# A four-stage residual block on one core: five exchanges of order, and the copies of the key pages moved to later unit steps

## The chip, the core and the metric

One NeuronCore of a Trainium2 chip runs the whole program. The metric is the device time in microseconds, the median of several executions. Each profiled execution is a single one; its span runs from the first to the last instruction.

## What is computed

x has shape (8, 128, 512). Four stages are added to it, one after the other. The part of the reference that matters here:

```
x = x + L0(x)   # SwiGLU MLP, F = 1376, with LoRA adapters of rank 16 per sequence
x = x + L1(x)   # attention: 32 query heads, 8 key heads, D = 128, 512 cached keys
                # gathered from pages by block_table, and 128 new keys
x = x + L2(x)   # 512 x 512 weight, quantised by a codebook, with LoRA
x = x + L3(x)   # 512 x 512 weight chosen per sequence

q = rope(rmsnorm(x Wq)); k = rope(rmsnorm(x Wk)); v = x Wv
kc = k_cache[block_table]; vc = v_cache[block_table]        # 16 pages of 32 keys
probs = softmax(where(valid, q k^T * D**-0.5, -1e30)); o = probs v
out = o Wo
```

## The kernel before

Every fp32 product is made of three products in the faster fp32r format: each operand is split into a high half (ScalarE, ACT, copies it with rounding) and a low half (VectorE, DVE, or GpSimd, POOL, subtracts). TensorE (PE) multiplies high by high, high by low and low by high.

Each of the five engines runs its own instruction list, written out by hand as Python calls in the order of issue, and waits for counts of semaphores. Nothing is scheduled by a tool, so the order of the calls is the order on the engine. The fifth engine, SP, computes nothing: it issues DMAs, one after the other, and a wait in its list holds back all that stand behind.

**The MLP** works in 11 blocks of the hidden width for each half of the sequences. For a block n, `high_w(n)` and `low_w(n)` split the weights, `high_wb` and `low_wb` the adapters, `silu` and `gated` make the activation and `high_act`, `low_act` split it. `mask_t` and `low_t` prepare the products of the adapters (tile `tb`), for which TensorE waits in `lora_out`. `angles` makes the rotary angles, which are needed later.

**The attention** works in 64 units: unit k is key head k // 8 of sequence k % 8, with its four query heads. The engines are software-pipelined: in step u, TensorE projects unit u (`project_q`, `project_kv`), turns and applies the probabilities of unit u - 2 (`transpose_p`, `attend`), makes scores of units u - 1 and u, and ends with `output(u - 2)`, which reads `oTh` and `oTl`. `transpose_queries` and `transpose_new` turn the rotated queries and the new keys. The first three units (`first`, `second`, `third`) are written out by hand, since they overlap the end of the MLP.

The probabilities are not divided by their sums; the output is. For this the four inverses of each row have to be laid across the partitions, and they go through DRAM: `invert` on DVE makes `inv`, SP's `put_inv` stores it in `inv_dram` (2 KB), SP's `spread_inv` waits for that store and broadcasts it to all partitions (`inv_row`, 256 KB), ACT's `lay_inv` copies it into the order of the output (`inv_wide`), DVE's `norm_o` multiplies, and ACT's `high_o` makes `oTh`. ACT has `square_q`, `scale_k` and `high_o` behind `lay_inv`, all in the order of the list.

The cached keys and values are first copied page by page from the cache into DRAM buffers in the order of the sequences (128 pages of 128 KB for the keys, on SP; `copy_keys(n)` issues the next n). Each page has its index read from SBUF into registers, and then its DMA. Units 0 to 7 wait for the 16 pages of their sequence in `load_k`; later heads read the same buffers. 92 of the 128 pages are issued before the first unit step of SP, `step(0)`, and the rest between the other DMAs of the steps 0 to 6: `load_v`, `load_rope`, `load_k` (four DMAs), and in step 4 four weight loads of the next head (`load_next_in`). The DVE engine turns the loaded keys in `turn_cached_k`, ACT makes their high half in `high_cached_k`.

**The last two stages** go sequence by sequence; `add3(b)` adds the third stage's result into x, after which TensorE turns it (`turn_x3`), and `low_w3_part` splits a quarter of the last weights.

Of the kernel before, what the change touches and what calls it, by code (L numbers as in the profile page):

```python
# [24 lines left out]
B, T, HID = 8, 128, 512  # L25
# [17 lines left out]
KC = KEYS // P  # L43
SPLIT = KEYS // 2
PUT_SCALES = 32
QW = REP * D
QKV = QW + 2 * D
DEPTH = 4
# [80 lines left out]
def cond_resid_kernel(nc, ins, out):  # L129
    ctx = ExitStack()  # L130
    with ctx:
# [218 lines left out]
        def _(sp):  # L350
# [153 lines left out]
            first = Unit(0)  # L504
# [38 lines left out]
            def spread_inv(u):  # L543
                if u.exists():
                    sp.wait_ge(S["inv_put"], u.count(16, 16))
                    sp.dma_start(inv_row[:, :], inv_dram[u.k % 2].rearrange("t h -> (t h)").partition_broadcast(P)
                                 ).then_inc(S["inv_in"], 16)

            def step(u):
                put_inv(u + -2)  # L550
                if u.k == 2:
                    spread_inv(u + -2)
                    copy_keys(2)
                else:
                    if u.k < B - 1:
                        copy_keys(2)
                    spread_inv(u + -2)
                if (u + -1).exists() and u.k > 1:
                    load_v(u + -1)
                if (u + 1).exists():  # L560
                    load_rope(u + 1)
                    load_k(u + 1)
                load_next_in(u)
                load_next_out(u)
                if u.k < B - 1:
                    copy_keys(4 if u.k else 2)

            def load_w3(b):
                if b >= 2:
# [15 lines left out]
            for n in range(2):  # L585
                cols = slice(n * HID // 2, (n + 1) * HID // 2)
# [188 lines left out]
        def _(act_e):  # L775
# [168 lines left out]
            for n in range(1, FC):  # L944
                if n >= 3:
                    high_w(n + 1)
                high_act(n - 1)
                if n == FC - 1:
                    copy_delta(0)
                if n >= 3:  # L950
                    high_wb(n + 1)
                if n == 7:
                    sines()
                    act_e.wait_ge(S["idx_in"], 64)
                    act_e.activation(scales[:, 0, :], scales[:, 0, :], ACT.Exp).then_inc(S["scale_exp"], 1)
                if FC - 3 <= n < FC - 1:
                    split_wd(n - (FC - 3))
                silu(n)
                if n == 1:
                    high_wb(3)  # L960
                if n == 2:
                    angles()


            high_x(1, 0)
# [12 lines left out]
            for m in range(1, FC):  # L978
                n = FC + m
# [15 lines left out]
            first = Unit(0)  # L995
# [222 lines left out]
            square_k(third)  # L1218
            high_pt(first, 1)
            high_pt(first, 2)  # L1220
            high_pt(first, 3)
            high_pt(first, 4)
            exp(second, 0)
            lay_inv(first)
            high_cached_k(third)
            square_q(third)
            scale_k(third)
            run_steps(step, 3, UNITS)


# [69 lines left out]
        def _(pe):  # L1300
# [211 lines left out]
                    delta(1 + m // 3)  # L1512


            def project(u, cols, width, name):

                b = u.seq
                if cols == 0 and u.k < B:
# [3 lines left out]
                if cols == 0 and u.new_head():  # L1522
# [10 lines left out]
                    i.then_inc(S[name], 1)  # L1533
                    return
                for c in range(C):
                    if u.k == 0 and cols == 0:
                        pe.wait_ge(S["wqkv_h"], c + 1)
                        pe.wait_ge(S["wqkv_l"], c + 1)
                    split = ((xh, wh), (xh, wl), (xl, wh))
                    if cols and u.new_head() and c >= 2:  # L1540
                        pe.wait_ge(S["w_low_pool"], 6 * u.head - 5 + c)
                    for a, w in split:
                        i = mm(proj_ps[:, 0:width], a[:, b, c, :], w[:, c, cols:cols + width], start=k == 0, stop=k == 3 * C - 1)  # L1543
                        k += 1
                i.then_inc(S[name], 1)

            def project_q(u):
                if not u.exists():
                    return
                if u.back(3):  # L1550
                    pe.wait_ge(S["y_added"], (u + -3).count(1, 1))
                elif u.k >= 1:
                    pe.wait_ge(S["k_copied"], u.count(1, 0))
                    pe.wait_ge(S["vnl_set"], u.count(1, 0))
                else:
                    pe.wait_ge(S["act_f"], 2 * FC)
                project(u, 0, QW, "q_done")

            def project_kv(u):
                if not u.exists():  # L1560
# [143 lines left out]
                if k == 9:  # L1704
                    project_kv(first)
            transpose_queries(first)
            project_q(second)
            transpose_new(first)
            turn_x1(4)
            scores(first, 0)  # L1710
            scores(first, 1)
# [130 lines left out]
        def _(dve):  # L1842
# [235 lines left out]
            low_la(1)  # L2078
            low_w(2)
            low_wb(0)  # L2080
            low_wb(1)
            dve.wait_ge(S["iota_set"], 6)
            mask_t(0, 0)
            mask_t(0, 1)
            low_t(0, 0)
            low_t(0, 1)
# [274 lines left out]
            mean_square_q(second)  # L2361
            low_q(second)
            low_new_k(second)
            invert(first)
            low_x1(7)
            low_pt(first, 0)
# [3 lines left out]
            mask_max(second, 1)  # L2370
            shift(second, 0)
            low_pt(first, 3)
            turn_cached_k(third)
            low_pt(first, 4)
            low_new_v(third)
            mean_square_k(third)
            norm_o(first)
            mask_max(second, 2)
            low_o(first)
# [76 lines left out]
            for b in range(1, B - 1):  # L2456
# [4 lines left out]
                if b + 2 < B:  # L2461
                    low_w3(b + 1)
            low_w3_part(B - 1, 0)
            low_w3_part(B - 1, 1)
            add3(B - 1)
            low_w3_part(B - 1, 2)
            low_x3(B - 1)
            low_w3_part(B - 1, 3)
# [65 lines left out]
```

## Time and profile before

| | before |
|---|---|
| median of 3 runs (1372.57 to 1373.29) | 1372.97 us |
| profiled execution | 1375.03 us |
| its span | 1373.4 us |
| PE busy | 1364.4 us, 99% |
| DVE busy | 1014.7 us, 74% |
| ACT busy | 978.2 us, 71% |
| POOL busy | 750.2 us, 55% |
| granted clock of TensorE | 1.00 |

The span is the time from the first to the last instruction of the profiled execution; what lies around it is launch and end. "Busy" counts each engine's instructions in flight. TensorE's matmuls are pipelined, and the ends of its instructions are modelled, so its idle time is best read together with the distance between the starts of its instructions.

### The profile page before, as it was taken

How to read it: one execution, taken by the hardware profiler on the slowest of the kernel's cores; microseconds unless marked ns; L12 is line 12 of the kernel's file. 1: busy time of each engine (PE TensorE's matmuls, PEld its weight loads, DVE VectorE, ACT ScalarE, POOL GpSimd, SP SyncE). 2: the span in 40 equal slices, each digit the busy share in tenths (PEclk: the TensorE clock that was granted, in tenths of full speed). 3: DMA queues.
4: the chain of work that ended last, by engine and by line, in shares of the span. 5: the costliest groups of instructions: out<-in, count | busy, mean ns of one | idle time of the engine just before them, and what ended most of it. 6: DMA issues, size and time to landing. Idle time of an engine off the chain costs nothing.

```text
span 1373.4 us, 26359 instructions
## 1 busy us (share of the span) xinstructions
PE 1364.4 (99%) x7842; PEld 1188.1 (87%) x7842; DVE 1014.7 (74%) x2115; ACT 978.2 (71%) x1990; POOL 750.2 (55%) x990
## 2 busy tenths in 40 slices
PE   9999999999999999999999999999999999999998
PEld 7888878888888888888888888888888888888887
DVE  5887776777777777777777777777777777777776
ACT  5767665666777777777777777777777767777853
POOL 5421324666765576557655665666566656665600
DMA  7877889574424233424242324232424242433344
GB/s 196 261 260 222 279 271 297 128 177 120 96 63 109 66 98 70 113 64 96 66 108 63 93 62 108 62 93 62 108 62 94 62 108 63 94 67 67 86 156 153
DMA packets 256739, 165.80 MB, mean 121 GB/s; under 512 B 157413, under 2 KB 223846, under 8 KB 251094
## 3 DMA queue, kind: packets, MB, share of 16 engines
q1 hardware_dynamic: 249952, 142.48, 39.4%
q0 software_dynamic: 5376, 19.60, 5.3%
q10 hardware_dynamic: 1270, 2.04, 0.4%
q8 instruction: 64, 1.05, 0.3%
q14 instruction: 77, 0.63, 0.2%
HBM read 158.66 MB, written 38.94 MB: 144 GB/s over the span
## 4 chain that ended last, share of the span: by engine, by line
PE 94%; DMA 2%; ACT 1%; issue 1%; SPq 1%; DVE 1%; POOLq 0%; POOL 0%; ACTq 0%; DVEq 0%
PE proj_ps L1543 18%; PE sc L1580 16%; PE o_ps L1620 16%; PE ring L1598 10%; PE sc L1317 9%; PE proj_ps L1636 4%; PE proj_ps L1639 4%; PE proj_ps L1647 4%; PE proj_ps L1317 4%; PE o_ps L1317 3%; PE ring L1659 2%; PE ring L1409 1%; DMA inv_dram<-inv 1%; PE ring L1672 0%; PE proj_ps L1526 0%
## 5 line engine op out<-in xcount | busy, mean ns | idle before, releaser
L2233 DVE TENSOR_TENSOR pTl<-ring,pTh 128x512 fp32r<-128x512 f32 x320 | 215.3, 689 | 135.4 <-ACT pTh L1045 131.3
L1034 ACT ACTIVATE p_sb<-p_sb,bias,rstd 128x640 f32<-128x640 f32 x254 | 233.5, 920 | 50.6 <-DVE bias L2216 50.5
L746 POOL TENSOR_TENSOR rstd<-var,half_neg 128x4 f32<-128x4 f32 x64 | 65.1, 1016 | 297.3 <-DVE var L2265 297.3
L2200 DVE CUSTOM_DVE_ANT_0 p_sb<-sc,mask 128x640 f32<-128x640 f32 x254 | 204.4, 823 | 27.3 <-PE sc L1580 21.4
L1045 ACT ACTIVATE pTh<-ring 128x512 fp32r<-128x512 f32 x320 | 184.4, 599 | 27.1 <-PE ring L1598 25.5
L1598 PE MATMUL ring<-ident,p_sb 128*128 128x128 f32 x1270 | 180.7, 272 | 0.7 <-ACT p_late L1034 0.6
L1598 PEld LDWEIGHTS ring<-ident,p_sb 128*128 128x128 f32 x1270 | 151.8, 140 | 27.3 <-DVE pTl L2233 0.9
L1543 PE MATMUL proj_ps<-wh,xh 128*128 128x256 f32 (+1 forms) x484 | 169.1, 349 | 0.0
L1580 PE MATMUL sc<-kTh,qTh 128*128 128x320 f32 x512 | 162.7, 318 | 0.5 <-DVE kTl L2307 0.5
L1543 PE MATMUL proj_ps<-wl,xh 128*128 128x256 f32 (+1 forms) x484 | 161.8, 334 | 0.0
L1543 PE MATMUL proj_ps<-wh,xl 128*128 128x256 f32 (+1 forms) x484 | 161.4, 333 | 0.0
L1580 PE MATMUL sc<-kTh,qTl 128*128 128x320 f32 x512 | 158.0, 309 | 0.0
L1580 PE MATMUL sc<-kTl,qTh 128*128 128x320 f32 x512 | 157.8, 308 | 0.0
L1081 ACT ACTIVATE q_sb<-proj_ps 128x512 f32<-128x512 f32 x64 | 38.2, 597 | 166.9 <-PE proj_ps L1543 158.6
L654 POOL DMA_DIRECT2D v_pages<-in_v_cache x128 | 64.9, 507 | 137.7 <-issue 133.7
L700 POOL TENSOR_TENSOR q_sin<-q_sb,rope 128x256 f32<-128x256 f32 x128 | 91.7, 736 | 76.3 <-issue 72.5
L1620 PE MATMUL o_ps<-pTh,vh 128*128 128x512 f32 x256 | 116.9, 457 | 0.0
L1580 PEld LDWEIGHTS sc<-kTh,qTh 128*128 128x128 f32 x512 | 96.3, 188 | 6.1 <-issue 0.7
L1620 PE MATMUL o_ps<-pTl,vh 128*128 128x512 f32 x256 | 101.5, 397 | 0.0
L1543 PEld LDWEIGHTS proj_ps<-wh,xh 128*128 128x128 f32 x484 | 91.3, 189 | 11.5
L1620 PE MATMUL o_ps<-pTh,vl 128*128 128x512 f32 x256 | 100.9, 394 | 0.0
L1580 PEld LDWEIGHTS sc<-kTl,qTh 128*128 128x128 f32 x512 | 96.3, 188 | 5.1
(281 smaller groups left out, 3635.9 us busy)
## 6 DMA issues: line engine op xcount, KB each, us to landing
v_pages<-in_v_cache POOLq DMA_DIRECT2D x128, 128.0 KB, 4.0
k_pages<-in_k_cache SPq DMA_DIRECT2D x128, 128.0 KB, 3.7
k_raw<-k_pages SPq DMA_DIRECT2D x256, 64.0 KB, 2.8
v_raw<-v_pages SPq DMA_DIRECT2D x64, 256.0 KB, 4.5
rope<-rope_dram SPq DMA_DIRECT2D x64, 256.0 KB, 4.0
inv_row<-inv_dram SPq DMA_DIRECT2D x64, 256.0 KB, 4.4
stage<-in_Wqkv SPq DMA_DIRECT2D x32, 384.0 KB, 5.1
w_raw<-in_WguT SPq DMA_DIRECT2D x19, 512.0 KB, 5.4
```

Of the source, the lines that this page charges most:

```text
L654: pool.dma_start(v_pages[b, j * PSIZE:(j + 1) * PSIZE, :, :].rearrange("s h d -> s (h d)"), ins["v_cache"][bass.ds(pg, 1), :, :, :].rearra ...
L700: pool.tensor_tensor(dst[:, :, s, :], src[:, :, 1 - s, :], tab[:, 1, s * 64:(s + 1) * 64].unsqueeze(1).to_broadcast([P, REP, 64]), ALU.mul ...
L746: pool.tensor_tensor(rstd[:, u.k % 2, 0:REP], var[:, u.k % 2, 0:REP], half_neg[:, 0:REP], ALU.pow).then_inc(S["q_pow"], 1)
L1034: act_e.activation(weights_of(u, h), weights_of(u, h), ACT.Exp, bias=bias[:, h:h + 1], scale=rstd[:, u.k % 2, h:h + 1], accum_out=total[:, ...
L1045: act_e.activation(pTh[:, c, :], ring[c % 2][:, :], ACT.Copy).then_inc(S["pth"], 1)
L1317: i = mm(out, a, b, start=start and k == 0, stop=stop and k == last)
L1543: i = mm(proj_ps[:, 0:width], a[:, b, c, :], w[:, c, cols:cols + width], start=k == 0, stop=k == 3 * C - 1)
L1580: i = mm(score_ps[h % 2][:, s, 0:SPLIT], a[:, par, hs], w[:, par, ks], start=k == 0, stop=k == 2)
L1598: i = nc.tensor.transpose(ring[c % 2][:, h * P:(h + 1) * P], weights_of(u, h)[:, c * P:(c + 1) * P], ident[:, :])
L1620: i = mm(o_ps[:, :], a, w[:, c, :], start=c == 0 and k == 0, stop=c == KC - 1 and k == 2)
L2200: v.tensor_tensor_reduce(out=weights_of(u, h).rearrange("p (s k) -> p s k", s=2), in0=score_ps[h % 2][:, :, 0:SPLIT], in1=mask[:, u.seq, : ...
L2233: v.tensor_tensor(pTl[:, c, :], ring[c % 2][:, :], pTh[:, c, :].bitcast(F32), ALU.subtract).then_inc(S["ptl"], 1)
```

## The change

Five places exchange neighbours in the order of an engine. On SP, the broadcast of the inverses is always issued before the pages of a step, and the number of pages behind the loads of step k is read from a table, 2, 0, 4, 7, 7, 6 in place of 2, 4, 4, 4, 4, 4, 4, with no page in step 6.

```diff
+KEYS_AFTER = (2, 0, 4, 7, 7, 6)
@@ SP, step(u)
                 put_inv(u + -2)
-                if u.k == 2:
-                    spread_inv(u + -2)
+                spread_inv(u + -2)
+                if u.k < B - 1:
                     copy_keys(2)
-                else:
-                    if u.k < B - 1:
-                        copy_keys(2)
-                    spread_inv(u + -2)
                 if (u + -1).exists() and u.k > 1:
                     load_v(u + -1)
...
-                if u.k < B - 1:
-                    copy_keys(4 if u.k else 2)
+                if u.k < B - 2:
+                    copy_keys(KEYS_AFTER[u.k])
@@ ACT, the first half of the MLP: for n in range(1, FC)
                 if n >= 3:
                     high_w(n + 1)
                 high_act(n - 1)
+                if n == 3:
+                    angles()
...
                 if n == 1:
                     high_wb(3)
-                if n == 2:
-                    angles()
@@ ACT, the first units
             high_pt(first, 2)
+            high_cached_k(third)
             high_pt(first, 3)
             high_pt(first, 4)
+            lay_inv(first)
             exp(second, 0)
-            lay_inv(first)
-            high_cached_k(third)
+            scale_k(third)
             square_q(third)
-            scale_k(third)
@@ TensorE
+                    if c == 2 and between:
+                        between()
...
-            project_q(second)
-            transpose_new(first)
+            project_q(second, lambda: transpose_new(first))
@@ DVE, the start of the MLP
             low_wb(0)
-            low_wb(1)
             dve.wait_ge(S["iota_set"], 6)
             mask_t(0, 0)
+            low_wb(1)
             mask_t(0, 1)
@@ DVE, the first units
             low_new_k(second)
+            turn_cached_k(third)
             invert(first)
...
-            turn_cached_k(third)
             low_pt(first, 4)
+            mean_square_k(third)
             low_new_v(third)
-            mean_square_k(third)
@@ DVE, the last sequence
             low_w3_part(B - 1, 0)
+            add3(B - 1)
             low_w3_part(B - 1, 1)
-            add3(B - 1)
```

The pages issued in the steps 0 to 6 are so 4, 6, 6, 6, 6, 6, 2 before, and 4, 2, 6, 9, 9, 6, 0 now (128 in all, so the last call of either version has fewer than its number).

The first place is SP in step 3, from the store of the inverses of unit 1 on; a page is four rows, of which the last is its DMA. Before:

```order
L541 DMA inv_dram<-inv 128x4
L389 TENSOR_LOAD idx
L389 ISA x2
L352 ISA
L352 DMA k_pages<-in_k_cache 16x2048
L389 TENSOR_LOAD idx
L389 ISA x2
L352 ISA
L352 DMA k_pages<-in_k_cache 16x2048
L546 DMA inv_row<-inv_dram 128x512
L486 DMA v_raw<-v_pages 128x4x128
```

The same place now:

```order
L542 DMA inv_dram<-inv 128x4
L547 DMA inv_row<-inv_dram 128x512
L390 TENSOR_LOAD idx
L390 ISA x2
L353 ISA
L353 DMA k_pages<-in_k_cache 16x2048
L390 TENSOR_LOAD idx
L390 ISA x2
L353 ISA
L353 DMA k_pages<-in_k_cache 16x2048
L487 DMA v_raw<-v_pages 128x4x128
```

The broadcast (`inv_row`) has moved ahead of the two pages, right behind the store on which it waits. The second place is ACT in the first units, from the high halves of the turned probabilities of unit 0 (`pTh`) to its output (`oTh`). Before:

```order
L1045 ACTIVATE pTh<-ring 128x512 x4
L1034 ACTIVATE p_sb,total<-p_sb,bias,rstd 128x640
L1061 ACTIVATE inv_wide<-inv_row 128x512
L1133 ACTIVATE kTh<-k_turned 128x512
L1088 ACTIVATE sq_q<-q_sb 128x512
L1120 ACTIVATE k_cos<-k_cos,rstd 128x128
L1071 ACTIVATE oTh<-o_ps 128x512
```

The same place now:

```order
L1042 ACTIVATE pTh<-ring 128x512 x2
L1130 ACTIVATE kTh<-k_turned 128x512
L1042 ACTIVATE pTh<-ring 128x512 x2
L1058 ACTIVATE inv_wide<-inv_row 128x512
L1031 ACTIVATE p_sb,total<-p_sb,bias,rstd 128x640
L1117 ACTIVATE k_cos<-k_cos,rstd 128x128
L1085 ACTIVATE sq_q<-q_sb 128x512
```

The cached keys of unit 2 (`kTh`) come two instructions earlier, the inverses (`inv_wide`) ahead of the exponential, and the scaling of the new keys (`k_cos`) ahead of the squares; `oTh` follows these rows in both. The third place is DVE at the start of the MLP, from the low halves of the adapters (`wb`) to the product tiles (`tb`). Before:

```order
L1910 TENSOR_TENSOR wb<-lb,wb 32x256 x4
L1924 TENSOR_TENSOR prep<-ring,own 32x512 x2
L1931 TENSOR_TENSOR tb<-prep,tb 32x512 x2
L1894 TENSOR_TENSOR w_l<-w_raw,w_h 128x1024
L2056 TENSOR_TENSOR e_sb<-sc,e_sb 128x512
```

The same place now:

```order
L1908 TENSOR_TENSOR wb<-lb,wb 32x256 x2
L1922 TENSOR_TENSOR prep<-ring,own 32x512
L1908 TENSOR_TENSOR wb<-lb,wb 32x256 x2
L1922 TENSOR_TENSOR prep<-ring,own 32x512
L1929 TENSOR_TENSOR tb<-prep,tb 32x512 x2
```

The first masked product (`prep`) no longer stands behind the second block's adapters.

## Rows read from the trace of the kernel before

**Rows 1.** The page, busy time of each engine, its share and instructions.

```profile
PE 1364.4 (99%) x7842; PEld 1188.1 (87%) x7842; DVE 1014.7 (74%) x2115; ACT 978.2 (71%) x1990; POOL 750.2 (55%) x990
```

**Rows 2.** Waits of PE: us in total, times, longest.

```profile
PE sc L1317 <- DVE x3T_l L2421: 0.7, 1, 0.7
PE ring L1672 <- ACT k_cos L1120: 0.6, 1, 0.6
PE sc L1389 <- DVE tb L1931: 0.6, 1, 0.6
...
PE sc L1580 <- DVE kTl L2307: 0.5, 1, 0.5
PE proj_ps L1636 <- ACT oTh L1071: 0.4, 2, 0.3
PE o_ps L1317 <- issue: 0.4, 1, 0.4
PE ring L1779 <- DVE x_sb L2391: 0.3, 1, 0.3
...
PE sc L1389 <- DVE wb L1910: 0.2, 1, 0.2
```

**Rows 3.** PE in order of time near 268 us: start, us, instruction, [idle].

```profile
267.82 0.31 PE L1580 MATMUL sc<-kTh,qTl 128*128 128x320 f32 x1
268.77 0.33 PE L1672 MATMUL ring<-ident,k_cos 128*128 128x128 f32 x1 [0.64 <-ACT k_cos L1120]
```

**Rows 4.** SP's queue in order of time, steps 2 to 4: start, us.

```profile
263.21 0.34 SPq L546 DMA_DIRECT2D inv_row<-inv_dram  x1
...
267.43 2.22 SPq L478 DMA_DIRECT2D k_raw<-k_pages  x4
270.42 4.72 SPq L352 DMA_DIRECT2D k_pages<-in_k_cache  x4
...
281.08 3.69 SPq L478 DMA_DIRECT2D k_raw<-k_pages  x4
285.54 4.34 SPq L352 DMA_DIRECT2D k_pages<-in_k_cache  x4
291.63 0.35 SPq L541 DMA_DIRECT2D inv_dram<-inv  x1
...
300.49 2.45 SPq L490 DMA_DIRECT2D stage<-in_Wqkv  x4
303.71 4.29 SPq L352 DMA_DIRECT2D k_pages<-in_k_cache  x4
308.04 0.58 SPq L541 DMA_DIRECT2D inv_dram<-inv  x1
```

**Rows 5.** Issue to landing (last), issued at 275.19, 291.63, 263.21, 279.49.

```profile
inv_dram<-inv SPq DMA_DIRECT2D x1, 2.0 KB, 4.3
inv_dram<-inv SPq DMA_DIRECT2D x1, 2.0 KB, 1.4
inv_row<-inv_dram SPq DMA_DIRECT2D x1, 256.0 KB, 3.0
inv_row<-inv_dram SPq DMA_DIRECT2D x1, 256.0 KB, 4.5
```

**Rows 6.** ACT and PE in order of time: the inverses and output products.

```profile
284.00 1.14 ACT L1061 ACTIVATE inv_wide<-inv_row 128x512 f32<-128x512 f32 x1 [1.52 <-DMA inv_row<-inv_dram]
286.62 0.73 PE L1636 MATMUL proj_ps<-woh,oTh 128*128 128x512 f32 x2 [0.29 <-ACT oTh L1071]
303.35 0.94 PE L1636 MATMUL proj_ps<-woh,oTh 128*128 128x512 f32 x3
320.12 1.17 PE L1636 MATMUL proj_ps<-woh,oTh 128*128 128x512 f32 x4
```

**Rows 7.** DVE in order of time: the reciprocals of units 0 and 1.

```profile
258.33 0.18 DVE L2226 RECIPROCAL inv<-total 128x4 f32<-128x4 f32 x1 [1.07 <-ACT p_sb L1034]
274.24 0.18 DVE L2226 RECIPROCAL inv<-total 128x4 f32<-128x4 f32 x1 [0.47 <-ACT p_sb L1034]
```

More of the change, by code:

```diff
@@ L1512, in _, with project @@
                     delta(1 + m // 3)
-            def project(u, cols, width, name):
+            def project(u, cols, width, name, between=None):
                 b = u.seq
@@ L1545, in project, with project_q @@
                 i.then_inc(S[name], 1)
-            def project_q(u):
+            def project_q(u, between=None):
                 if not u.exists():
@@ L1556, in project_q @@
                     pe.wait_ge(S["act_f"], 2 * FC)
-                project(u, 0, QW, "q_done")
+                project(u, 0, QW, "q_done", between)
             def project_kv(u):
```

## Prediction

> **What bounds the kernel now.** I read four views. The page first: TensorE (PE) is busy for 1364.4 of 1373.4 us [rows 1], so the reader is to see that only about 9 us of the span are TensorE's to give, and that no busy time of another engine matters unless TensorE waits for it. Then the waits of TensorE by length [rows 2]: those that the change touches are 0.6 (tb), 0.2 (wb) and 0.4 us (put down to issue) in the first 41 us, then 0.5 (kTl), 0.6 (k_cos) and 0.4 us (oTh, in two pieces) between 245 and 287 us, and 0.3 us (x_sb) at the end. From 287 us to the tail TensorE has no wait: a unit takes 16.77 us, the distance between the starts of two output products, 303.35 and 320.12 [rows 6]. Third, TensorE in order of time: idle time is counted from the modelled end of the last product, and a restart costs more than that. The product of 320 columns that starts at 267.82 has a modelled length of 0.31 us, but where nothing waits the next one starts after half of that, while it drains; here the next starts at 268.77 [rows 3], which is 0.80 us too late where the view says 0.64. So I add 0.16 us to each wait. Fourth, the order of time on the SP queue between 258 and 313 us [rows 4], since the largest piece of the change is there.
>
> **The small exchanges.** (1) low_wb(1) stands behind mask_t(0, 0), and angles() behind high_w(4) and high_act(2). The waits for tb, wb and the one at 40 us hang on the DVE and ACT queues of that stretch: the eight angle instructions stood ahead of the split of the fourth weight block. Behind high_act(2) they run while TensorE works on the fourth block, and what follows them on ACT is 0.4 us or so later than in the order of before at worst, ahead of its reader. Gain 0.6 + 0.2 + 0.4 plus 3 x 0.16 = 1.65 us; bounds 0.6 (tb alone) and 1.65. (2) transpose_new(first) runs after six of the twelve products of project_q(second), so kTh, then kTl, are there when the first scores begin. Gain 0.5 + 0.16, less one more change of weights, which I bound by 0 and 0.1: 0.6. (3) Unit 2's cached keys are turned, split and scaled ahead of square_q, and lay_inv(first) ahead of exp(second, 0). The k_cos wait (0.6 + 0.16) goes, and the first of the two oTh waits, if inv_row for unit 0 lands before high_pt(first, 4) has ended. It landed 3.0 us after its issue at 263.21 [rows 4, 5]; without the four pages of step 1 in front (about 5.0 us of SP) SP waits for DVE's reciprocal, done at 258.51 [rows 7], so the put goes out at about 258, the broadcast at about 259.5, and inv_row is there at about 262.5. exp(second, 0), now later by lay_inv's 1.1 us [rows 6], has nobody waiting for it before the next unit. Gain 0.8 + 0.3 = 1.1. (4) The second oTh wait, at 286.62, comes from lay_inv at 284.00, which had waited for inv_row [rows 6]; with the broadcast ahead it goes: 0.5. (5) At the end add3(7) stands one low_w3_part earlier; the wait for x_sb goes, 0.3 + 0.16 = 0.45. low_x3 behind it waits for ACT and moves with it, so the 0.7 us wait for x3T_l only shifts. Sum of the small ones: 1.65 + 0.6 + 1.1 + 0.5 + 0.45 = 4.3 us; with nothing against it the median would be 1368.7.
>
> **The pages.** Pages per unit step were 4, 6, 6, 6, 6, 6, 2 and become 4, 2, 6, 9, 9, 6, 0. A page costs SP 1.26 us (four of them take 4.29 us from the first issue to the end of the last at 303.71, [rows 4]; (4.29 - 0.5)/3). SP had little to spare: in step 3 the pages ended at 289.88 (285.54 + 4.34) and the put went out at 291.63, 1.75 us later; in step 4 they ended at 308.00 and the put went out at 308.04, with no room at all, because that step also issues four weight loads (300.49, 2.45 us). Three pages more in each of these two steps are 3.8 us each. That is the term against the change.
>
> I follow SP on the clock of before, leaving out the 1.65 us by which everything shifts. What is known: before, the order of the new step stood once, in step 2: from the issue of the broadcast at 263.21 to the first late page at 270.42 are 7.2 us [rows 4]. Put of unit 1: its reciprocal was done at 274.42 [rows 7], now 1.7 us earlier, 272.7. No page has been issued for about 1.5 us by then (four late pages from 266.7 to 271.2), which is the state of the put at 291.63: it landed after 1.4 us, where the put right behind pages, at 275.19, took 4.3 [rows 5]. Broadcast at 274.1. First late page 281.3, seven pages 8.1 us, end 289.4. Put of unit 2 at 289.5; its reciprocal is ready at 291.6 - 2.2 = 289.4, so nothing is lost yet, but it is right behind pages: 4.3 us, broadcast at 293.8. First late page 7.2 + 2.5 us (weights) later, 303.5; seven pages, 311.6. Put of unit 3 at 311.7, where the reciprocal is ready at 308.04 - 2.2 = 305.8 or before: 5.9 us late. 4.3 us to land: broadcast at 316.0, landing after 3.0 [rows 5] at 319.0.
>
> What is late next: lay_inv(3) heads ACT's queue, with square_q, scale_k, oTh and the high half of the queries behind it, and DVE's norm_o waits for it; TensorE waits for oTh. At 284.00 lay_inv was the last thing to come and the output product started 2.62 us later, at 286.62 [rows 6]. So the output product of unit 3 starts at 319.0 + 2.6 = 321.6, against 320.12 before and 317.9 with the gains of the middle. The stall is 3.7 us. In step 5 the count is as before: broadcast 316.0, first late page 323.2, four pages, put at 327.6, broadcast 331.9, inv_row at 334.9; 2.6 us more are 337.5, and the output product of unit 4 has its place at 321.6 + 16.8 = 338.4, so nothing more is lost. Step 6 has no page. The loads of values, tables and keys go out some 4 us later; they are for the unit step after, so I take this at nothing and bound it by 1 us.
>
> Sum: -1.65 at the start, +1.5 over the middle (-2.2 + 3.7), -0.45 at the end: -0.6 us. The profiled execution took 1375.03 us with a span of 1373.4; the median shown is 1372.97, 2.1 below it, and what lies around the span doesn't change. 1372.97 - 0.6 = **1372.4 us**. A measurement of this kernel tells no change from 0.2%, 2.7 us.
>
> **The bounds of SP's chain.** Unknown are the issue of the four k_raw loads (2.22 us at 267.43, 3.69 at 281.08, [rows 4]; I take the first, since it stood in the order of the new step), the landing of the broadcast (3.0 or 4.5, [rows 5]; the first for the same reason), and the landing of the puts (1.4 or 4.3; the second, since pages end 0.1 us ahead of them). Worst: 2 x 1.5 + 1.5 = +4.5 us, 1376.9; with the start's gain at its lower bound, 1378. Best: one put at 1.4 takes 2.9 us off, so that 0.8 of the stall is left, 1369.5; both take all of it, 1368.7.
>
> The page "DMA: Bandwidth & Descriptors" of the Trainium skill (section on queues, rings and completion order) says that the semaphore of a DMA is raised only after every earlier write of the same DMA engine has landed. By that rule the 2 KB put counts as landed after the pages issued ahead of it, and this trace's 4.3 against 1.4 us agrees with it.
>
> **The rivals.** A, the forecast: SP falls behind in step 4 and most of the gain is given back. B: the stall doesn't appear, because the two puts land in 2 us or less though pages are just ahead. Then the put of unit 3 goes out at 309.4 at the latest, the broadcast at 311.4, inv_row at 314.4, before lay_inv's place; all 4.3 us stay: 1368.7. Against it stands the row of 4.3; for it the row of 1.4, and that only two puts are shown. The same page's section on the anatomy of one DMA gives a fixed cost of about 2.0 us that scales with nothing, though for the path of GpSimd; by it B would hold, and the trace has both smaller and larger numbers. C, on the other side: the k_raw loads are issued at 3.7 us in steps 3 and 4 and the broadcast lands after 4.5: the output product of unit 3 then starts at 326.1, 1376.9. It decides (over 1375.7) once the landing of inv_row for unit 3 is 3.3 us later than 319.0. For it: values, tables and keys share the queue, and four weight loads stand there in step 4. Against: in step 2 the same order gave the low numbers. D: the waits at the start stay, because they hang on DMA landings that don't move: 1.65 us less gain, 1374.0 with A.
>
> **How the numbers follow.** A 0.52 (its own range 1371.0 to 1375.0), B 0.22, C 0.16, D 0.10. The range for 8 in 10 takes B in and most of C: 1368.6 to 1376.3. Faster by over 0.2% (below 1370.2): B and 0.06 of A, 0.28. Slower by over 0.2%: C, less what ends short of it, and a little of D, 0.17. The rest, 0.55, within.
>
> **What would show it.** Right: in the profile after, TensorE's waits for tb, wb, kTl, k_cos and x_sb are gone; a new wait for oTh of 3 to 4 us stands near 316 to 320 us, with inv_wide waiting for the landing of inv_row; SP's put of unit 3 follows a page with no wait for DVE. Wrong: no such wait (then B), or waits for oTh in three units (then C). If the waits at 27 to 40 us are still there, step (1) is wrong.

## The result, and the profile after

The changed kernel takes 1378.6 us (median of 7 runs, 1374.67 to 1380.16), the kernel before on the same chip 1373.18 us (median of 7, 1372.57 to 1374.71). The ratio is 1.0034, 95% interval 1.0024 to 1.0044: slower by 5.4 us, where I had forecast 0.6 us less, and outside my range. One caution for all that follows: the profiled execution of the changed kernel took 1374.67 us (span 1373.0) and is the fastest of its seven, so its trace shows the mildest form of what happens.

The page of the changed kernel, busy time of each engine, beside [rows 1]:

```profile
span 1373.0 us, 26359 instructions
...
PE 1362.2 (99%) x7842; PEld 1186.8 (86%) x7842; DVE 1012.5 (74%) x2115; ACT 978.1 (71%) x1990; POOL 752.5 (55%) x990
```

TensorE's idle time is 10.8 us, where it was 9.0. The waits of TensorE in the changed kernel (total, times, longest), beside [rows 2]:

```profile
PE ring L1671 <- ACT k_cos L1117: 2.1, 1, 2.1
PE ring L1459 <- DVE e_sb L2067: 1.7, 1, 1.7
PE o_ps L1386 <- DVE wb L1908: 1.4, 1, 1.4
PE sc L1314 <- DVE x3T_l L2419: 0.7, 1, 0.7
PE proj_ps L1635 <- ACT oTh L1068: 0.6, 2, 0.3
...
PE ring L1406 <- DVE lad_l L2031: 0.5, 1, 0.5
```

The waits for tb, kTl, x_sb and the k_cos wait near 268 us are gone, as forecast. New are wb (1.4, where 0.2 stood before) and lad_l (0.5) at the start, one of the two for oTh (0.3, near 301 us), and k_cos (2.1) with the other oTh (0.3) near 320 us. One of the four waits that went is no gain that the exchange can be shown to have made: the runs e3, e9, e10 and e11 below keep the old order at the start, and their traces have no wait for tb either, so the 0.6 us are seen in one execution of the old order out of five.

**The start.** ACT and TensorE in order of time in the changed kernel:

```profile
35.70 0.63 ACT L848 ACTIVATE act_h<-e_sb 128x512 fp32r<-128x512 f32 x1
37.74 0.26 ACT L853 ACTIVATE lad_h<-lad 128x64 fp32r<-128x64 f32 x1 [1.41 <-PE ring L1406]
37.91 2.01 ACT L777 ACTIVATE prep<-nw,small 128x64 f32<-128x64 f32 x8
39.82 1.68 ACT L836 ACTIVATE wb<-lb 32x256 fp32r<-32x256 f32 x4
...
42.53 0.47 PE L1386 MATMUL o_ps<-tb,wb 96*128 96x256 f32 x2 [1.40 <-DVE wb L1908]
```

The second copy of high_act(2), lad_h, waits 1.41 us for a product of TensorE that frees its buffer. The eight angle instructions now stand behind that wait and no longer run in its time; wb comes behind them, DVE splits it, and TensorE stands for 1.40 us. At the adapter product that starts at 73.62 us TensorE is 0.12 us ahead of the same product before (73.74). But the two executions did not begin alike: the first adapter product starts at 26.74 and at 27.33. From that first one to this one, in all profiled executions (the runs e1 to e12 are explained below):

| order at the start | kernels | us |
|---|---|---|
| as before | before, e3, e9, e10, e11 | 46.41, 45.85, 45.32, 45.21, 45.62 |
| as changed | changed, e1, e2, e4, e7, e8 | 46.88, 46.88, 46.90, 46.92, 46.91, 47.05 |
| angles() one place earlier | e5, e6, e12 | 45.13, 45.10, 45.09 |

So of the 1.65 us forecast nothing is there. By the means, 46.92 against 45.68, the changed start is 1.2 us slower, and the kernel before showed the slowest of its five.

**The middle.** The output products of the units 0 to 4, whose distance is a unit's time, beside [rows 6]:

```profile
267.00 1.20 PE L1635 MATMUL proj_ps<-woh,oTh 128*128 128x512 f32 x4
283.77 1.17 PE L1635 MATMUL proj_ps<-woh,oTh 128*128 128x512 f32 x4
301.23 1.19 PE L1635 MATMUL proj_ps<-woh,oTh 128*128 128x512 f32 x4 [0.29 <-ACT oTh L1068]
320.86 1.19 PE L1635 MATMUL proj_ps<-woh,oTh 128*128 128x512 f32 x4 [0.29 <-ACT oTh L1068]
337.59 1.17 PE L1635 MATMUL proj_ps<-woh,oTh 128*128 128x512 f32 x4
```

Unit 2 starts its output at 301.23, before it was 303.35: 2.0 us gained over the middle beside the start's 0.1, where 2.2 were forecast. (Not all of that is the change: e9, e10 and e11 are the kernel before up to here, and start it at 301.06 to 301.96, as their start was faster.) Then unit 3 takes 320.86 - 301.23 = 19.63 us in place of 16.77: a stall of 2.9 us. SP's queue over steps 3 to 5, beside [rows 4]:

```profile
283.64 8.17 SPq L353 DMA_DIRECT2D k_pages<-in_k_cache  x7
291.85 0.87 SPq L542 DMA_DIRECT2D inv_dram<-inv  x1
294.05 0.34 SPq L547 DMA_DIRECT2D inv_row<-inv_dram  x1
...
298.27 2.42 SPq L479 DMA_DIRECT2D k_raw<-k_pages  x4
300.73 2.65 SPq L491 DMA_DIRECT2D stage<-in_Wqkv  x4
304.14 8.10 SPq L353 DMA_DIRECT2D k_pages<-in_k_cache  x7
312.28 0.58 SPq L542 DMA_DIRECT2D inv_dram<-inv  x1
314.72 0.33 SPq L547 DMA_DIRECT2D inv_row<-inv_dram  x1
```

The put of unit 3 goes out at 312.28 right behind the last page (forecast 311.7), its broadcast at 314.72 (forecast 316.0; the put landed 2.4 us after its issue, and not 4.3). What hangs on it, on ACT:

```profile
318.27 1.11 ACT L1058 ACTIVATE inv_wide<-inv_row 128x512 f32<-128x512 f32 x1 [3.79 <-DMA inv_row<-inv_dram]
```

The output product follows 2.59 us later, at 320.86, where I had counted 2.62. TensorE waits for k_cos, which stands behind lay_inv on ACT, and hardly for oTh, for which I had forecast the whole wait. From first to last instruction this execution is 0.4 us shorter than before, and I had 0.6; that the two are near is partly luck, since the profiled execution of before is 2.1 us over its median and several terms were off against each other. The six others are longer: their spans are 1374.5 to 1378.5 us, and in five of them the mean granted clock of TensorE is 0.998 or 0.999. What the clock does there was not in my sum at all.

### The profile page after: what moved, and what is told of

Its sections match the earlier page's. It is cut to its first block, busy times and chain, and to the rows that moved or that the text cites. A ratio compares the mean times of both kernels' runs of the same rounds, so it can differ in the third digit from the quotient of the medians.

```text
span 1373.0 us, 26359 instructions
## 1 busy us (share of the span) xinstructions
PE 1362.2 (99%) x7842; PEld 1186.8 (86%) x7842; DVE 1012.5 (74%) x2115; ACT 978.1 (71%) x1990; POOL 752.5 (55%) x990
## 4 chain that ended last, share of the span: by engine, by line
PE 94%; SPq 2%; DMA 1%; ACT 1%; issue 1%; DVE 1%; DVEq 0%; ACTq 0%
PE proj_ps L1542 18%; PE sc L1579 15%; PE o_ps L1619 15%; PE ring L1597 10%; PE sc L1314 9%; PE proj_ps L1635 4%; PE proj_ps L1638 4%; PE proj_ps L1646 4%; PE proj_ps L1314 4%; PE o_ps L1314 3%; PE ring L1658 2%; PE ring L1406 1%; PE ring L1336 1%; SPq L353 1%; DMA inv_dram<-inv 1%
```

## The experiments

The first four ran on one chip, beside it the kernel before at 1374.3 us (median of 23).

**e1: the changed kernel again.** No edit, to have a profile of an execution from the middle of the distribution.

> The changed kernel once more, for the spread of its runs. Its profiled run showed a span of 1373.0 us and a clock of 1.000, while six other runs had spans of 1374.5 to 1378.5, most at 0.999. Theory A (SP's chain varies: landings of the puts and of the broadcast make the stall for unit 3 longer in most runs): median 1377 to 1379, and where the trace is of a run over 1376, its waits for k_cos and oTh near 318 us add up to 5 us or more. Theory B (the stall is always about 3 us, and the granted clock falls behind it): same median, but the waits stay near 3 us and a stretch after 320 us shows a clock below 1. Theory C (the start of the MLP varies): the difference lies before 230 us.

Measured: 1379.61 us (5 runs, 1377.27 to 1380.21), ratio 1.0035 [1.0021, 1.0049]. The profiled execution has a span of 1378.1. Its longest wait, the output products around it, and TensorE's windows (busy us, instructions, granted clock, DMA share, GB/s):

```profile
PE ring L1671 <- ACT k_cos L1117: 4.2, 1, 4.2
```

```profile
302.16 1.17 PE L1635 MATMUL proj_ps<-woh,oTh 128*128 128x512 f32 x4
323.87 2.07 PE L1635 MATMUL proj_ps<-woh,oTh 128*128 128x512 f32 x4
342.64 1.17 PE L1635 MATMUL proj_ps<-woh,oTh 128*128 128x512 f32 x4
359.39 1.17 PE L1635 MATMUL proj_ps<-woh,oTh 128*128 128x512 f32 x4
```

```profile
315.00:320.00 5.00, 4.04 (x25) 1.00 0.42 78
320.00:325.00 5.00, 1.60 (x4) 0.64 0.93 246
325.00:330.00 5.00, 5.00 (x20) 0.68 0.50 103
330.00:335.00 5.00, 5.00 (x32) 1.00 0.28 54
```

The granted clock stands at 0.50, which is 1.2 of 2.4 GHz, for 6.8 us, from about 321 to 328 us. The fall begins while TensorE still waits for k_cos, and for some 5 us it then works at half speed: the four output products take 2.07 us in place of 1.17. In the intervals: unit 3 takes 21.71 us (+4.9 over 16.77), unit 4 takes 18.77 (+2.0), unit 5 16.75. So the pages cost this execution 6.9 us, the profiled execution above 2.9. The page "TensorE: Matmul & The Clock Gate" of the Trainium skill (part 1, on the clock gate) has a table of two states of the array's clock, 1.2 GHz when TensorE has idled and 2.4 GHz when it is busy. The rows agree on the two levels; that not every wait brings the clock down is seen in the profiled execution above, which waited 2.1 and 0.3 us and kept 1.00.

The longer wait comes from SP: put 3 went out at 314.66, the broadcast at 317.38, and inv_wide started at 321.27. Counted from the output product of unit 2 that is 2.1 us later than in the first profile. The four k_raw loads of step 4 took 3.77 us to issue (2.42 there), put 2 landed in 2.8 us (2.2), and 0.6 us more lie between put 3 and inv_wide; the weight loads took 0.7 us less. That is part of my rival C. Of the theories on record it lies between A and B: the waits are longer than 3 us but do not add up to 5, and the clock falls.

**e2: the exchanges alone.** The pages and the place of the broadcast as before, all else as changed.

```diff
-                spread_inv(u + -2)
-                if u.k < B - 1:
+                if u.k == 2:
+                    spread_inv(u + -2)
                     copy_keys(2)
+                else:
+                    if u.k < B - 1:
+                        copy_keys(2)
+                    spread_inv(u + -2)
...
-                if u.k < B - 2:
-                    copy_keys(KEYS_AFTER[u.k])
+                if u.k < B - 1:
+                    copy_keys(4 if u.k else 2)
```

> All five exchanges, pages and broadcast as before. If the pages own all of the loss: 1371.5 to 1372.7 (the start gives about 0.1, because wb of the fourth block is 1.4 us late behind angles; kTl gives 0.6, the end 0.45; the k_cos wait stays, since lay_inv(first) now stands ahead of exp and waits for inv_row). If the exchanges carry the loss: 1375 or more.

Measured: 1373.91 us (11 runs), ratio 0.9996 [0.9987, 1.0005], clock 1.000 in all. TensorE waits 1.4 us for wb, 0.9 for lad_l and 0.7 for oTh in unit 0. The exchanges alone don't make the kernel slower, and as they stand they give nothing that can be told: the start loses 1.2 us by the table above, which eats what the others give. The median is above the 1371.5 to 1372.7 that I had expected (the kernel before is 1.3 us higher on this chip than my base), and the wait for k_cos, which I had expected to stay, went, while one of 0.7 us for oTh came.

**e3: the pages and the broadcast alone.** The other half: step() and the table as changed, all exchanges undone.

> Only the change on SP, every exchange undone. If the pages own the loss: 1377 to 1380, with the wait for k_cos of 2 us or more near 320 us. If the exchanges are needed for it: 1372 to 1374.

Measured: 1378.01 us (7 runs), ratio 1.0027 [1.0016, 1.0039]. Its longest wait, and TensorE's windows behind it:

```profile
PE ring L1669 <- ACT k_cos L1117: 3.3, 1, 3.3
```

```profile
320.00:325.00 5.00, 3.80 (x9) 0.52 0.87 185
325.00:330.00 5.00, 5.00 (x24) 0.80 0.40 109
```

The stall and the lower clock come with the pages alone (inv_wide waited 4.96 us for the landing of inv_row and started at 319.08).

**e4: the change without the later pages.** The broadcast ahead in every step and all exchanges, but the old counts.

```diff
-KEYS_AFTER = (2, 0, 4, 7, 7, 6)
+KEYS_AFTER = (2, 4, 4, 4, 4, 4)
```

> All of the change, broadcast ahead of the pages too, but the number of late pages is 2, 4, 4, 4, 4, 4 and two in step 6, as before. If three pages more in steps 3 and 4 cause the stall: no wait for k_cos or oTh over 0.5 us near 320 us and a median of 1369.8 to 1371.3. If the order of the broadcast is to blame (its put no longer has pages to hide behind): 1374 or more, with the stall still there.

Measured: 1373.2 us (11 runs), ratio 0.9991 [0.9982, 1.0000], 6.4 us below the changed kernel on the same chip. No wait near 320 us, clock 1.000, as the first theory had it, though the median is not in its 1369.8 to 1371.3, even with 1.3 us added for the chip. So the place of the broadcast is harmless, and the loss is the counts. What stays open: which of the steps.

The next four ran together, beside the kernel before at 1374.15 us (median of 33).

**e7 and e8: three pages more in one step only.** Against the changed kernel:

```diff
-KEYS_AFTER = (2, 0, 4, 7, 7, 6)
+KEYS_AFTER = (2, 3, 4, 7, 4, 4)      # e7, step 3
+KEYS_AFTER = (2, 3, 4, 4, 7, 4)      # e8, step 4
```

> The changed kernel with the counts 2, 3, 4, 7, 4, 4 behind the loads: three pages more in step 3 alone, one fewer in step 1, none in step 6. Theory (SP has 3.3 us of room in step 3, and the loss needs step 4 as well): no wait for k_cos near 320 us, granted clock 1.000, time within 0.5 us of the run with the old counts (0.999 of before). Rival (the delay of step 3 is handed on in full to step 4): put of unit 2 at 292 us or later, inv_wide of unit 3 waits 2 us or more for inv_row, 1.0015 or more.

> The changed kernel with the counts 2, 3, 4, 4, 7, 4 behind the loads: three pages more in step 4 alone, one fewer in step 1, none in step 6. Theory (step 4 has no room, so its three pages of 1.26 us make the put of unit 3 3.5 us late, at about 311.3 us, its broadcast at 313.8, inv_wide at 317.5 to 318 in place of 316.3 to 317.3): a short wait of TensorE of 1 to 1.5 us near 320 us, too short to bring its granted clock down, 1.000 throughout, and 1 to 1.5 us slower than the run with three more in step 3. Rival (step 4 alone is the whole of the loss): a wait of 3 us and more with the clock at half behind it, 1.0025 and more.

Measured: e7 1374.27 us (11 runs), ratio 1.0004 [0.9995, 1.0013]; e8 1372.67 us (11 runs), ratio 0.9989 [0.9980, 0.9998]. SP and ACT in e8:

```profile
301.50 8.10 SPq L353 DMA_DIRECT2D k_pages<-in_k_cache  x7
309.64 0.58 SPq L542 DMA_DIRECT2D inv_dram<-inv  x1
312.86 0.33 SPq L547 DMA_DIRECT2D inv_row<-inv_dram  x1
```

```profile
316.33 1.13 ACT L1058 ACTIVATE inv_wide<-inv_row 128x512 f32<-128x512 f32 x1 [0.74 <-DMA inv_row<-inv_dram]
```

In these two profiled executions neither step alone stalls TensorE by more than 0.3 us near 320, and e8 refutes the short wait of 1 to 1.5 us that I had expected of it, and with it the order of the two: it is the faster one. The seven pages of step 4 start at 301.50, where they start at 304.14 in the changed kernel, since put 2 had gone out at 290.24 and not at 291.85 and landed sooner (1.6 us against 2.2), and inv_wide at 316.33 is still in time. In e7 SP enters step 4 late (put 2 at 293.38), but with four pages there put 3 goes out at 310.46. The large stall needs both steps: the second has no time in which to make good the delay of the first. That step 3 alone is harmless isn't shown. In e7 unit 2 took 17.37 us, 0.6 more than 16.77, and its profiled execution (1373.72 us) is one of the faster; five of its eleven runs took 1375.28 to 1377.23, one with a mean clock of 0.999, while the slowest of e8 took 1374.79. These may make the 1.6 us between the medians, but they have no trace. By the ratios e7 is 1.8 us above e4, where I had expected at most 0.5. (Both have three pages behind the loads of step 1, where the changed kernel has none.)

**e5: the old counts and angles() one place earlier.** As e4, with the eight angle instructions behind high_w(4) and ahead of high_act(2):

```diff
                 if n >= 3:
                     high_w(n + 1)
-                high_act(n - 1)
                 if n == 3:
                     angles()
+                high_act(n - 1)
```

> The changed kernel with the page counts of before (2, 4, 4, 4, 4, 4 behind the loads, two in step 6) and with angles() one place earlier on ACT: behind the high half of w of chunk 4 and ahead of high_act(2). Theory (the start's gain was lost because angles() stands behind a copy that waits for TensorE, so that the high half of wb of chunk 4 comes 1.4 us late): the waits for wb (1.4 us) and most of lad_l (0.5 to 0.7) are gone from TensorE's list, and the kernel is 1.5 to 2 us faster than the same with angles() behind high_act(2), which stood at 0.9991 of before; so about 0.998. Rival (the stall only moves to the next copies of ACT, as w_h or act_h are then late by the 2.0 us of angles()): a new wait of 1 to 2 us for act_h or w_h in the same place and the ratio stays at 0.999.

Measured: 1371.81 us (11 runs), ratio 0.9983 [0.9974, 0.9992]. This is faster than both kernels: 2.3 us below before, and about 7 us below the changed kernel by the ratios ((1.0034 - 0.9983) x 1373). The wait for wb is gone; near 267 us stand one of 0.6 us for k_cos and one of 0.7 us for oTh (e4 has the second too). ACT in e5:

```profile
36.26 2.01 ACT L777 ACTIVATE prep<-nw,small 128x64 f32<-128x64 f32 x8
38.17 0.62 ACT L848 ACTIVATE act_h<-e_sb 128x512 fp32r<-128x512 f32 x1
38.69 0.25 ACT L853 ACTIVATE lad_h<-lad 128x64 fp32r<-128x64 f32 x1
38.84 1.69 ACT L836 ACTIVATE wb<-lb 32x256 fp32r<-32x256 f32 x4
```

The angles fill the time in which lad_h would have waited, lad_h finds its buffer free, and wb starts at 38.84 in place of 39.82, though TensorE began later here (first adapter product at 27.53 against 26.74).

**e6: another table.** As e5, but the four pages of step 1 moved to the steps 2 and 3, two each.

```diff
-KEYS_AFTER = (2, 4, 4, 4, 4, 4)
+KEYS_AFTER = (2, 0, 6, 6, 4, 4)
```

> As the kernel before in this batch, with the counts 2, 0, 6, 6, 4, 4 behind the loads and two pages in step 6: the four pages leave step 1, as in the change, but go to the steps 2 and 3, and the steps 4 and 5 stay at four. Theory (SP has no room in step 4 alone; step 3 has 3.3 us between its last page and its put in the run with the old counts, and step 2 is served by the earlier start): the wait for oTh of unit 0 (0.7 us) is gone as in the change, no wait near 320 us, 0.5 to 1 us faster than the run before in this batch, 0.9975 of the kernel before. Rival (two pages more in step 2 or 3 make the next put late as in step 4): inv_wide of unit 1 or 2 waits for inv_row and TensorE waits 1 us or more near 285 or 302 us.

Measured: 1373.43 us (11 runs), ratio 0.9994 [0.9985, 1.0003], 1.6 us slower than e5, where I had expected 0.5 to 1 us faster. The oTh wait of unit 0 went, but inv_wide now waits for its broadcast in the units 2 to 4:

```profile
297.87 1.14 ACT L1058 ACTIVATE inv_wide<-inv_row 128x512 f32<-128x512 f32 x1 [2.19 <-DMA inv_row<-inv_dram]
315.39 1.14 ACT L1058 ACTIVATE inv_wide<-inv_row 128x512 f32<-128x512 f32 x1 [1.68 <-DMA inv_row<-inv_dram]
332.62 1.15 ACT L1058 ACTIVATE inv_wide<-inv_row 128x512 f32<-128x512 f32 x1 [1.35 <-DMA inv_row<-inv_dram]
```

Once SP is behind, it stays behind for three units, in short waits of TensorE (0.6 and 0.3 us near 300, 0.3 near 318, 0.2 near 335). They cost more than their length: the units 2 to 4 take 18.08, 17.53 and 17.23 us, together 2.5 over three times 16.77, against some 1.4 that come in earlier. So two pages more in each of the steps 2 and 3 are not free, as the rival had it, though its wait of 1 us and more in one place didn't come.

The last four ran together, beside the kernel before at 1373.5 us (median of 21).

**e9, e10, e11: a stall without any moved page.** Is it the pages, or the wait, that brings the clock down? The kernel before, with ACT made late once by repeating the copy of the inverses of unit 3 (the result is unchanged; ident_set is only a counter for the copies):

```diff
                 act_e.wait_ge(S["inv_in"], u.count(16, 16))
+                if u.k == 3:
+                    for i in range(2):        # e10: 3, e11: 5
+                        act_e.activation(inv_wide[...], inv_row[...], ACT.Copy).then_inc(S["ident_set"], 1)
+                        act_e.wait_ge(S["ident_set"], i + 3)
```

> The kernel before, with ACT made late once: ahead of inv_wide of unit 3 it writes the same copy 2 times more, each waiting for the one before, estimated at 1.3 us each (1.12 us and the wait), 2.6 us in all. From the rows of before the high half of k_cos ends 1.2 us, and that of the output 0.6 us, ahead of their use, so TensorE waits about 1.6 us near 320 us. Both theories (a stall costs only its length; a long stall also brings TensorE's granted clock down) give the same here, since the wait of 2.1 us in the profiled run of the changed kernel kept 1.00: clock 1.00 and 1.5 to 2 us over before.

> As e9_hold_2 with 3 copies more, about 3.9 us on ACT and a wait of TensorE of about 2.9 us, no change on SP. Theory (behind a wait of about this length and more the granted clock is at half for some us, as behind the 3.3 and 4.2 us in the two runs with pages moved; the cause is the wait and not the pages): granted clock below 1.00 behind the wait, and 1.5 to 3.5 us over before beside the wait's own 3, so 4.5 to 6.5 us in all. Rival (the clock fell for something else in those runs, such as the transfers): 1.00 throughout and 3 us over before.

> As e9_hold_2 with 5 copies more, about 6.5 us on ACT and a wait of TensorE of about 5.5 us. Theory (clock at half behind a long wait): granted clock 0.50 for about 7 us behind it, 8.5 to 9.5 us over before, so some 3 us over the wait's own length. Rival (the stall costs its length alone): 1.00 throughout and 5.5 us over before.

Measured: e9 1375.2 us (10 runs), ratio 1.0011 [1.0002, 1.0021]; e10 1377.0 us (6 runs), 1.0031 [1.0019, 1.0044]; e11 1379.61 us (4 runs), 1.0050 [1.0034, 1.0066]. A copy cost 1.15 us and not 1.3, so the waits are shorter than planned. In each, 0.4 to 0.7 us of the k_cos waits listed are the old wait near 268 us. TensorE's windows in e9:

```profile
320.00:325.00 5.00, 5.00 (x28) 1.00 0.19 51
```

in e10, with its longest wait:

```profile
PE ring L1677 <- ACT k_cos L1125: 2.4, 2, 1.7
```

```profile
320.00:325.00 5.00, 4.13 (x11) 0.66 0.29 77
325.00:330.00 5.00, 5.00 (x28) 1.00 0.22 23
```

and in e11:

```profile
PE ring L1677 <- ACT k_cos L1125: 4.4, 2, 4.0
```

```profile
320.00:325.00 5.00, 2.75 (x8) 0.80 0.19 54
325.00:330.00 5.00, 5.00 (x25) 0.86 0.03 4
```

The clock falls with no page moved, so the wait is enough to cause it. By the medians they are 1.7, 3.5 and 6.1 us over before (by the ratios 1.5, 4.3 and 6.9; e10 and e11 have only six and four runs); I had expected 1.5 to 2, 4.5 to 6.5 and 8.5 to 9.5. The first held. In the other two the clock is at half for 3.4 us only, with the same loss of 1.6 us behind both, so the theory is right that there is such a term, and was wrong on its size.

**e12: the changed kernel with angles() one place earlier,** the edit of e5 with the counts of the change.

> The changed kernel with its own page counts and angles() one place earlier on ACT, ahead of high_act(2). Theory (the wait for wb of 1.4 us is the start's only, and the stall near 320 us is the pages' only): the wait for wb gone, the wait for k_cos of 2 to 5 us and the lower clock behind it as in the changed kernel, 1 to 1.5 us faster than the changed kernel and still over before: 1.002 to 1.003. Rival (the earlier start gives SP no more time, so the whole gain is eaten by a longer stall, as SP's pages don't shift with TensorE): 1.0035 as the changed kernel, with the wait for k_cos longer by about 1.4 us.

Measured: 1376.5 us (9 runs), ratio 1.0022 [1.0012, 1.0032], against 1.0034 and 1.0035 for the changed kernel in two measurements: 1.6 to 1.8 us less, though the intervals overlap; the table on the start has the same 1.8 us (45.09 against 46.9). The wait for wb is gone, the stall stays (k_cos 3.5 us, clock at half to 327 us):

```profile
319.34 1.11 ACT L1058 ACTIVATE inv_wide<-inv_row 128x512 f32<-128x512 f32 x1 [5.20 <-DMA inv_row<-inv_dram]
```

The two defects show up apart: the wait for wb can be taken away and the stall stays. In this profiled execution lad_l was late in three chunks (2.1 us in all, e5 had 0.4), for which I have no cause.

The starts of the output products of the units 2, 3 and 4 in these profiled executions, and what each interval is over 16.77 us; the second excess is half-clock alone, since nothing waits there, and the first has about 0.5 us of it beside the wait in e1, e3 and e12:

| kernel | unit 2 | unit 3 | unit 4 | excess of unit 3 | excess of unit 4 |
|---|---|---|---|---|---|
| before | 303.35 | 320.12 | 336.88 | 0 | 0 |
| changed | 301.23 | 320.86 | 337.59 | 2.9 | 0 |
| e1 | 302.16 | 323.87 | 342.64 | 4.9 | 2.0 |
| e3 | 300.83 | 321.68 | 340.89 | 4.1 | 2.4 |
| e12 | 300.89 | 321.93 | 341.12 | 4.3 | 2.4 |
| e9 | 301.39 | 319.45 | 336.18 | 1.3 | 0 |
| e10 | 301.96 | 321.20 | 339.53 | 2.5 | 1.6 |
| e11 | 301.06 | 322.58 | 340.92 | 4.8 | 1.6 |

## Why the prediction was wrong

Point by point, by its own steps.

- **What bounds it:** held. Every difference that I could place is a wait of TensorE or its clock, or a later begin of the execution; no busy time of another engine mattered.
- **(1) the start, 1.65 us:** failed, and this is the first of the two steps that made the forecast wrong. I said that behind high_act(2) the angles "run while TensorE works on the fourth block" and that what follows is late by 0.4 us at worst. I counted the copies' own durations and missed that lad_h, the second copy of high_act(2), waits for TensorE's product to free its buffer. Before, the angles filled that time. The wait moved to wb (1.4 us). The 0.6 us for tb were no gain either, as the old order has that wait in one of five executions only. The changed start is 1.2 us slower than the old one, so the term is off by 2.9 us (1.65 + 1.24). e5 and e12 show the cause by turning the two around: 1.8 us less than the changed start.
- **(2) and (3) the middle:** held. From the start to unit 0's output product the changed kernel needs 193.38 us (267.00 - 73.62), before 195.51 (269.25 - 73.74): 2.1 us where I had 0.6 + 1.1 (e1 has 193.81; the old order in e9, e10 and e11 195.12 to 195.53). **(4)** held too: the wait at 286.62 is gone. Unit 1 took 17.37 us before and 16.77 now, though the old order took only 16.84 to 17.28 in e9 to e11, so it is worth 0.1 to 0.6 us. Against them unit 2 needed 17.46 us, 0.7 more than its 16.77, as its inverses were late by 1.59 us already; that part of step 3's delay I had put at nothing.
- **(5) the end, 0.45:** held; the tail behind the last output product is 0.5 us shorter (1373.0 - 1318.91 against 1373.4 - 1318.77).
- **SP's chain, 3.7 us of stall:** the mechanism held, with its place, its put behind the last page at 312.28 for 311.7, and 2.59 us from inv_wide to the output product. The wait that I had named was the wrong one: TensorE stood for k_cos (2.1 to 4.2 us), which is also behind lay_inv, and for oTh only 0.3 us or not at all. The size was 0.8 high for the profiled execution (2.9) and low for the others: 4.9, 4.1 and 4.3 us. Parts of it were off in opposite senses. The puts right behind pages landed in 2.2 to 2.9 us, where I had taken 4.3; the broadcasts landed in 3.3 to 4.5 us, where I had taken 3.0, and the k_raw loads of the steps 3 and 4 took 2.1 to 4.2 us where I had 2.2. The row of 4.3 us on which I leaned is no constant of that position. Nor was the put of unit 1 free of pages, as I had taken it: it went out 0.16 us behind the last page and landed in 3.0 us, not in 1.4. The rule of completion order that I cited from the page "DMA: Bandwidth & Descriptors" of the Trainium skill isn't refuted by that, but it doesn't give the size.
- **What was missing altogether:** this is the second failed step. A stall was priced at its length, and the clock behind it at nothing. Behind waits of 3.3 to 4.2 us the granted clock was at 0.50 for nearly 7 us (e1, e3, e12), part of it while TensorE still waited, and the unit after lost another 2.0 to 2.4 us at 1.2 GHz. The three executions give a mean stall of 4.4 us (0.7 more than I had) and 2.3 of clock; with the 2.9 us by which the start is off, my 1372.4 becomes 1378.3. The kernel before was 0.2 and 1.3 us above the median that I started from on the two chips, so 1378.5 and 1379.6, against 1378.6 and 1379.6 measured. That the sum closes so well is luck in part: each term is a mean over a few executions that differ by more than what is left.
- **The rivals:** A won as to the mechanism, C as to the time and the sign. I had written that C decides from a landing 3.3 us later than 319.0. In e1 inv_wide started at 321.27, 2.3 us later, and in e12 at 319.34, hardly later, and both kernels are slower than before by over 0.2%, because the clock adds its part there (and in e1 the start). That point of decision was wrong for the missing terms, and so the 0.17 for slower was. The sign of being wrong that I had set for step (1), waits left at 27 to 40 us, missed the fault: those went, and the new one stood at 42.5 us.

**What stays open.** Why the time at half the clock is 6.8 us in the stalls with moved pages (e1, e3, e12) and only 3.4 us in those made by ACT (e10, e11), though e11's wait is as long as e1's. In the first three the clock falls while TensorE still waits, 2.3 to 2.6 us into the wait; in e10 and e11 it falls about 1 us after TensorE has gone on. The DMA share in the window with the stall was 0.87 to 0.93 in e1 and e3 and 0.19 to 0.29 in e10 and e11 (but 0.82 in the changed kernel's first profile, whose clock kept 1.00), and nothing was tried on it, and the stretch ahead of the wait differs as well. Also open is why the k_raw loads take 1.9 to 4.2 us to issue from one execution to the next. The changed kernel's times spread over 5.5 us where those of before spread over 2.1 on the same chip (but over 5.7 in 33 runs on another); that this issue time makes the spread is only argued, from the put times of e1 against the first profile.

## What to carry to other kernels

When TensorE is busy 99% of the time, price a stall twice: its length, and what TensorE loses at the lower clock behind it; here a wait of 4.2 us cost 6.9. Three pages more in a step that seemed to have no room cost nothing that could be told until the step ahead was late too. Before moving work behind another instruction, look at what that instruction waits for: the angles were free in front of a copy that would have waited anyway, and cost 1.8 us behind it. Before counting a short wait as a gain, look for it in a second execution of the same kernel: the wait for tb was in one of five. And where a queue runs without room, read the spread over several executions, since one profile may be the best of seven.

## What the runs showed of the hardware

- TensorE's granted clock was at 1.2 GHz (0.50) behind the longer waits and stayed at 2.4 GHz (1.00) behind the shorter, with one pair the other way round. The waits for k_cos and oTh together near 320 us, by the kernel: 1.00 throughout behind 2.1 + 0.3 us (the changed kernel's profiled execution) and behind those of e9 (0.6 + 0.3); below 1.00 behind those of e10 (1.7 + 0.3), e3 (3.3), e12 (3.5), e1 (4.2) and e11 (4.0 + 0.3). So 2.0 us brought it down in one execution, and 2.4 us did not in another.
- A 2 KB put issued within 0.1 us of the last of seven pages landed in 2.2 to 2.9 us (eight puts in the changed kernel, e1, e3 and e12) and in 2.2 and 3.2 us in e7 and e8. Puts as near behind three or four pages took 3.8, 4.3 and 4.4 us in the kernel before. Where pages were the last thing issued and 0.9 us or more lay between their end and the put, it landed in 1.4 us: 15 puts in ten traces, two of them in the kernel before.
- Four k_raw loads, of the same shape each time, took from 1.92 to 4.19 us to issue in the queue.
